# Lag matmuls and warm-up over all 128 rows, count tables one step later

## The reference

```python
ctx = causal_ema(x, tau_ctx)
wg = sigmoid(concat([x, ctx]) @ Wg.T + bg);  gated = x * wg
h1 = gelu(x @ Wn1.T + bn1)                       # 32 hidden units
mod = 0.5 + sigmoid(h1 @ Wn2.T + bn2)            # 32 traces
traces = causal_ema(gated * mod[d], tau_d)       # for each of the 32 traces d
temporal = sum over d of traces[d] * softmax(blend)[d]
out = (gelu(x @ Wsoma.T + bsoma) * sigmoid(temporal @ Wtemp.T + btemp)) @ Wout.T
x = x + layernorm(out) * gamma + beta
```

```python
s_scores = q . K[idx] * scale;  sparse_out = softmax(s_scores) @ V[idx]
dense_out = softmax(q . K * scale + lam * prior_bias) @ V
x = x + where(lam >= 1, sparse_out, dense_out) @ Wo.T + bo
```

## Time and profile before

| | |
|---|---|
| median of 3 runs | 340.48 us (339.88 to 341.51) |
| profiled execution | 342.68 us, its span from first to last instruction 340.8 us |
| mean granted TensorE clock over the span | 0.980 |
| TensorE busy | 318.4 us (93%) |
| VectorE busy | 277.4 us (81%) |
| GpSimd busy | 246.3 us (72%) |
| ScalarE busy | 214.9 us (63%) |
| share of the ending chain | TensorE 39%, VectorE 2%, ScalarE 2% |

### The profile page before, as it was taken

How to read it: one execution, slowest core, us unless ns; L and a number is a source line. 1 busy time by engine, 2 the same in 40 slices (tenths; PEclk the granted TensorE clock), 3 DMA queues, 4 the chain that set the end, 5 groups by cost and what they waited for, 6 DMA issues and landing times. The chain is left out here.

```text
span 340.8 us, 10005 instructions
## 1 busy us (share of the span) xinstructions
PE 318.4 (93%) x3333; PEld 212.4 (62%) x3333; DVE 277.4 (81%) x1453; ACT 214.9 (63%) x458; POOL 246.3 (72%) x298
## 2 busy tenths in 40 slices
PE   7998889999999999989987799999999999999995
PEld 2545355574746556565534576778878777878873
DVE  3895579897888789596788857899999999999982
ACT  5760225555555655644625788788888888888863
POOL 3154266768588676545536777799999999999990
PEclk9996799999999999997999999999999999999999
DMA  6600002023130603210551144565444345401011
GB/s 193 193 3 0 31 0 65 31 68 73 41 100 2 126 14 80 62 32 11 81 82 18 36 90 87 83 109 138 126 102 127 91 127 94 89 4 33 3 33 33
DMA packets 29154, 23.07 MB, mean 68 GB/s; under 512 B 2736, under 2 KB 27824, under 8 KB 29104
## 3 DMA queue, kind: packets, MB, share of 16 engines
q1 hardware_dynamic: 29104, 22.44, 29.0%
HBM read 7.75 MB, written 2.10 MB: 29 GB/s over the span
## 5 line engine op out<-in xcount | busy, mean ns | idle before, releaser
L1593 POOL TENSOR_TENSOR arena<-arena,neg_max 128x512 f32<-128x512 f32 x128 | 129.7, 1042 | 14.0 <-DVE neg_max L1435 13.5
L1435 DVE CUSTOM_DVE_ANT_0 arena<-ps,arena 128x128 f32<-128x128 f32 x512 | 113.7, 286 | 11.2 <-PE ps L765 5.5
L1080 ACT ACTIVATE arena<-ps 128x512 f32<-128x512 f32 x128 | 69.5, 596 | 9.1 <-PE ps L779 9.0
L779 PE MATMUL ps<-ident_sb,arena 128*128 128x128 f32 x512 | 68.2, 276 | 0.0
L1512 POOL TENSOR_TENSOR arena<-arena 128x448 f32<-128x448 f32 (+6 forms) x56 | 42.4, 757 | 31.2 <-DVE arena L1270 27.8
L779 PEld LDWEIGHTS ps<-ident_sb,arena 128*128 128x128 f32 x512 | 56.4, 141 | 7.0 <-issue 4.7
L1435 DVE DVE_READ_ACCUMULATOR2_ANT neg_max<- 128x1 f32 x512 | 42.4, 83 | 0.1
L795 PE MATMUL ps<-arena 128*32 128x128 f32 x1024 | 41.2, 279 | 0.0
L1499 POOL TENSOR_TENSOR arena<-decay_a,arena 128x192 f32<-128x192 f32 x32 | 19.4, 635 | 25.3 <-ACT arena L924 25.3
L1270 DVE SCALAR_TENSOR_TENSOR arena<-ps,lag_c,arena 128x448 f32<-128x448 f32 (+6 forms) x56 | 25.8, 484 | 8.5 <-POOL arena L1512 6.6
L795 PEld LDWEIGHTS ps<-arena 128*32 128x32 f32 x1024 | 24.1, 109 | 6.9 <-issue 0.3
(11 more groups left out here) (168 smaller groups left out, 594.3 us busy)
## 6 DMA issues: line engine op xcount, KB each, us to landing
arena<-q_parts SPq DMA_DIRECT2D x96, 64.0 KB
arena<-k_parts SPq DMA_DIRECT2D x96, 64.0 KB
arena<-in_x SPq DMA_DIRECT2D x16, 256.0 KB, 3.4
arena<-in_xt SPq DMA_DIRECT2D x8, 256.0 KB, 2.8
out<-arena SPq DMA_DIRECT2D x7, 256.0 KB, 3.0
arena<-in_consts SPq DMA_DIRECT2D x1, 420.0 KB, 3.9
w_sb<-in_w SPq DMA_DIRECT2D x1, 384.0 KB, 5.5
w_sb<-in_w SPq DMA_DIRECT2D x1, 192.0 KB, 4.2
```

The source lines that it names most:

```text
L779: mm = pe.transpose(ps[1][:, q % 2, k * P:k * P + P], neg_t[q % NT_RING][:, k * P:k * P + P], ident)
L1080: act.activation(probT[q % PT_RING], ps[1][:, q % 2, :], ACT.Exp, scale=-1.0)\
L1435: dve.tensor_tensor_reduce(out=neg_t[q % NT_RING][:, cs], in0=ps[0][:, score_bank(c) + slot, cs], in1=nbias[n % 2], scale=1.0, scalar=3.0e ...
L1593: pool.tensor_tensor(t4, t4, neg_max[:, n % 2, 4 * z:4 * z + 4].unsqueeze(2).broadcast_to([P, 4, P]), ALU.subtract).then_inc(s["shifted"], 1)
```

## The change

Four things change. The warm-up has twelve matmuls with operands of 128 rows instead of ten with 64, so `mod_pb[0]` is zeroed on all rows. The lag matmuls of group 0 contract all 128 rows. Since these hold four copies, `w_lag` is made a quarter as large (0.5 / NJ, with NJ = 4), and what is made of it for the other groups (`lag_a`, `w_rest`, the last block of `lag_b`) is multiplied by 4 again. In the front, VectorE does two of the three carries of group 0 ahead of lag 4, and the third behind lag 7. And `late_tables` moves from the end of step 5 into step 6, ahead of `b_temporal`.

```diff
@@ TensorE
             pe.wait_ge(s["half_set"], 1)
-            for _ in range(10):
-                pe.matmul(bank(1, 3), mod_pb[0][0:64, 0:P], mod_pb[0][0:64, :], start=True, stop=True)
+            for _ in range(12):
+                pe.matmul(bank(1, 3), mod_pb[0][:, 0:P], mod_pb[0][:], start=True, stop=True)
...
                     if at_start(i, m, 1):
-                        pe.matmul(bank(u, lag % 2), w_lag[0:D, lag, :], thd[u][0:D, :], start=True, stop=True)\
+                        pe.matmul(bank(u, lag % 2), w_lag[:, lag, :], thd[u], start=True, stop=True)\
@@ ScalarE
-                act.activation(lag_b[96:128], w_lag[96:128], ACT.Copy).then_inc(s["act_step"], 1)
+                act.activation(lag_b[96:128], w_lag[96:128], ACT.Copy, scale=float(NJ)).then_inc(s["act_step"], 1)
@@ VectorE
-            for n in range(2):
-                dve.memset(mod_pb[n][0:64, :], 0.0).then_inc(s["half_set"], 1)
+            dve.memset(mod_pb[0][:], 0.0).then_inc(s["half_set"], 1)
+            dve.memset(mod_pb[1][0:64, :], 0.0).then_inc(s["half_set"], 1)
...
-            pro("w_lag", dve.scalar_tensor_tensor(w_lag, half_bw[:].unsqueeze(1).broadcast_to([P, Q, P]), 0.5,
+            pro("w_lag", dve.scalar_tensor_tensor(w_lag, half_bw[:].unsqueeze(1).broadcast_to([P, Q, P]), 0.5 / NJ,
...
-                pro("w_a", dve.tensor_copy(lag_a[:], w_lag))
-                pro("w_rest", dve.tensor_tensor(w_rest, w_lag, lag_a[:], ALU.subtract))
+                pro("w_a", dve.tensor_scalar(lag_a[:], w_lag, float(NJ), None, ALU.mult))
+                pro("w_rest", dve.scalar_tensor_tensor(w_rest, w_lag, float(NJ), lag_a[:], ALU.mult, ALU.subtract))
...
-            def b_carries(i, m):
+            def b_carries(i, m, first=1, last=NJ):
...
-                for j in range(1, NJ):
+                for j in range(first, last):
@@ VectorE, front
-                b_carries(i, m)
+                b_carries(i, m, 1, NJ - 1)
                 f_lags(i, m, range(4, 6))
...
                 f_lags(i, m, range(6, Q))
+                b_carries(i, m, NJ - 1, NJ)
@@ VectorE, step
                 if first < last:
                     counts(first)
+                if 2 * i + m == COUNTED:
+                    late_tables()
                 b_temporal(i, m)
...
                 c_centre(i, m)
-                if 2 * i + m == COUNTED - 1:
-                    late_tables()
```

## The result

The changed kernel takes 335.45 us (median of 4 runs, 334.95 to 336.01), the kernel before 341.0 us beside it (4 runs); the ratio is 0.985, 95% interval 0.982 to 0.988. Three runs of this study (of the kernel before 345.82 us here and 346.6 us later, of the one with 64-row lags 344.58 us) were in a slower state and are left out of the ratios; without the first, the median of the kernel before is 340.48 us. Forecast were 333.9 us and a range of 332.2 to 337.1 us. The profiled execution took 335.92 us: 334.1 of span where the kernel before had 340.8.

The account below looks back on a forecast made before the run. Bounds: TensorE's lower clock in the front's chain, VectorE's tables in the chain into step 6. Warm-up 0.5, rows 3.28 and tables 3.01 less 0.15 made 6.6 us: 340.48 to 333.9 us, range 332.2 to 337.1.

Parts of the forecast that it names:

- the rival with a fall in a new place: Front: the clock falls after the lags, slowing L575 and L460 by 1.7 us, giving 335.6 us; chance 0.17.
- the terms are the same there: Whole kernel: the 6.6 us gain worked out on the profiled execution also holds for the median, 340.48 to 333.9 us.
- Rows, 3.28 us forecast: Lags of group 0: 128 rows keep the clock full, shortening lags 6 and 7, L564, L575 and L460 by 3.28 us.
- Warm-up, 0.5 forecast: Kernel start: full rows lift the clock before 9.5 us, so L455 and the transpose ahead are faster; 0.5 us.
- L1181's idle time of 0.48 us: Front, VectorE's wait for TensorE: taken as the most that a faster warm-up can hand on, 0.48 us.
- L1185 as a multiplication: Front, VectorE: scaling the lag table takes the cast's 0.69 us, no change; upper bound about 1.22 us.
- Third carry: Front, group 0: lags 6 and 7 start 0.7 us sooner but local matmuls wait; net 0, up to 0.7 lost.
- Tables, 3.01 less 0.15 forecast: Steps 5 and 6: moving them saves 2.27 us plus 0.74 for the step 6 fall, costing 0.15 ahead of L1299.
- one hold: Step 6, tables ahead of L1299: one table instruction is held beside GpSimd; near 2.0 us in all, 0.15 on the path.
- Rows do not move the clock: Front: contracted rows leave the clock as it was, only the tables pay 2.9 us, giving 337.6 us; chance 0.13.
- Slower: Attention stage: the clock falls there, beyond 17 us at the lower level, giving 342.2 us or more; chance 0.03.
- the prediction's list of marks: Observations named beforehand as showing it right or wrong, such as clock 1.00 over 24 to 40 us and L455 at 1.1 us.

Follow-up runs that it names:

- the second ratio: The whole changed kernel run again against the kernel before: 335.63 us (6 runs), ratio 0.987 (0.984 to 0.990).
- the 128-row filler: Kernel before plus one unread matmul of 128 rows ahead of lags 6 and 7 of group 0, lags kept at 32 rows: 338.45 us, ratio 0.994.
- the pair of extra matmuls: Kernel before plus one unread matmul ahead of lags 6 and 7 of group 0: with 32 rows 340.65 us, with 128 rows 338.45 us.

## Why the prediction was right, and where its sizes were off

The sign and the range were right. Of the mechanisms, the rows, the warm-up and the tables' move are shown by runs; that the move also takes away the fall in step 6 is not. The predicted time was 1.55 us too low. The gain was 5.0 us by the medians and 4.5 by the second ratio, for a forecast of 6.6. The pair of profiled executions hides this: 342.68 - 335.92 = 6.76 us. The forecast's own range, 332.4 to 335.2 us, missed 335.45; the stated range held because it takes in the rival with a fall in a new place (335.6). That the time lies next to that rival's is chance: no profile of the changed kernel has the fall in front that it describes.

**The step that failed** is the one from the profiled execution to the median, "the terms are the same there". The profiled execution of the kernel before had a clock of 0.980. It belongs to the heap of 15 in 69 executions whose median is 342.1 us; the other 54 have 340.3, and clocks above what both falls of the earlier trace rows leave: (10.3 + 3.4) / 2 us lost of 340 make 0.980. The new fall near 187 us is the smaller part: the six of ten executions of the changed kernel with a clock of 0.997 or more have a median of 335.0 us, still 1.1 above the forecast, and the other four 336.2. What a fall costs was summed rightly for that execution; for the median it had to be weighed by how many executions have it, and how long.

- **Rows, 3.28 us forecast, 2.0 measured alone** (0.8 either way), **2.0 to 2.4 taken back.** In the profiles it is exact: 4.40 - 1.13 = 3.27 us. In the median it is less. Many executions of the kernel before seem to have a shorter fall, by their clocks near 0.987 rather than 0.984; no profile is of such a one. But in the profiles of kernels with lags of 32 or 64 rows (without the 128-row filler) the first fall lasts about 10 us in four and 6.8 us in three, and with the tables alone, where it was 6.8, the gate product of group 1 came 1.48 us sooner. And while nothing else is changed with it, four of seven keep a fall of 3.4 us by their clocks, and the profile has it at 30.1 us. That is the rival of a new place, and it was true of this part alone; in all five profiles of kernels that have the rows part together with others, the clock is 1.00 there. The prediction's count of the stretch ahead of the fall is off by one (five of the eight matmul instructions are lag matmuls, not six), and the local matmuls are 1.13 of the 2.19 us ahead of the second fall; neither changes the argument.
- **Warm-up, 0.5 forecast, 1.2 alone, 0.9 taken back.** The profile of before had the rise at 10.8 us; where it comes at 11.8, L419 behind L455 is at the lower level too. The bound taken, L1181's idle time of 0.48 us, was none: the same wait is 1.24 us in the changed kernel with the 64-row warm-up. Of the 1.13 us between the two profiles some 0.5 is an input that was used 0.52 us sooner (VectorE's L1166 at 8.63 instead of 9.15 us). That isn't the change's: in the 13 other profiles, with either warm-up, L1166 starts at 8.61 to 8.81 us.
- **L1185 as a multiplication**: 0.69 us, as forecast. **Third carry**: 0 forecast, 0.4 us faster measured, with an interval that holds 0.
- **Tables, 3.01 less 0.15 forecast, 1.1 alone, 1.2 to 1.5 taken back.** The sum in the profiled pair came out: L1299's lead grows by 7.82 - 4.85 = 2.97 us. But it is 1.6 us from the move and 1.37 from the fall in step 6, which was called 0.74; and most executions of the kernel before seem, by their clocks, not to have that fall. Of the eight profiles with the tables in the old place only this one has it. Runs don't show that the move takes it away: with the tables alone moved, 3 of 12 executions have a clock of 0.981 to 0.983, about as many as the 15 of 69 before. In the tables' new place one hold was forecast and is there: L1226 took 1.07 us beside GpSimd's L1513, which started 0.16 us earlier and ended 0.16 us earlier too. The Trainium skill ("SBUF — State Buffer", SBUF: two separate sides) describes it: the two engines share ports under an exclusive lock, held for a whole instruction, and a VectorE instruction with two SBUF inputs needs it beside a GpSimd instruction that reads SBUF. The trace agrees.
- **Rows do not move the clock**, the rival with 0.13, is refuted by the pair of extra matmuls, twelve executions each. The Trainium skill's rule ("TensorE: Matmul & The Clock Gate", Part 1), that the gate follows how busy TensorE has been, isn't enough here: 100% busy with mostly 32 rows fell, 2.50 busy of 3.40 us with 128 rows did not the earlier trace rows. Whether it is the rows themselves or something that goes with them (the numbers multiplied, say) is open; only f32 lag and filler matmuls and the bf16 warm-up were varied.
- **Slower**, the rival by a fall in the attention stage: its mechanism exists, its size doesn't. 3.4 us at the lower level near 187 us cost 0.97 us in the profile; it needed 17 us at that level. The fall wasn't in the prediction's list of marks for this stage.

The part that stays open is why 4 of 10 executions of the changed kernel have a clock below 0.996 and 6 not. The two of the four that were profiled have their fall behind the thin stretch at 183 us, and the kernel before passes the same stretch at 190 us without one; that it depends on how the clock's own pace lies against the kernel fits, but is not shown.

## What to carry to other kernels

Give TensorE's small matmuls all 128 rows where the data allow it (copies with a scaled table do): the rows cost no time here (four f32 instructions of 512 columns took 1.98 us with 32 rows and 1.99 with 128), and only with 128 did the clock stay up. Ask of a fall in the profile how many executions have it before putting its price into a median: the mean clock of every run tells how much time was spent at the lower level, though not where. Short work that sits on a chain may be moved into idle time of the same engine elsewhere, and gains what it took less what it takes there (2.28 - 0.66 us).

## What was not expected of the hardware

- TensorE with no gap at all (3.90 of 3.90 us) lost its full clock, with most of its matmuls over 32 rows; one of 128 rows in place of one of 32 kept it over that place and brought 2.2 us by the medians (340.65 to 338.45).
- A warm-up of twelve matmuls with 64 rows, 5.30 us without a gap, didn't raise the clock until 11.8 us; with 128 rows it rose at 5.7 us, inside the warm-up.
- In 2 of 14 profiles TensorE stood still for 2.42 and 1.40 us amid equal matmuls, with no wait in the trace.
- Which of two engines was held changed between two executions that differ by 0.01 us in their order there. VectorE's L1252 took 1.13 us in the kernel before, with GpSimd's L1499 started 0.01 us ahead of it (54.15 and 54.16 us), and 0.69 us in the changed kernel, where both start at 49.75. There it was GpSimd's four additions that were longer, 2.80 us instead of the 2.24 that four take in step 5 before. VectorE's 0.44 us are as much as lies between the leads of 4.40 and 4.85.
